# The last batch of an attention written apart, its output summed by pairs, and the next stage's table computed before the barrier

## What is computed

```python
x = layernorm(x + attention(x, Wq, bq, Wk, bk, Wv, bv, Wo))   # 16 heads of 64, block-causal mask
logits = x @ router_w.T + router_b
topv, topi = top_k(logits, 2); gates = softmax(topv)            # 2 of 8 experts for each row
y = sum over experts e of gates[e] * down_e(silu(gate_e(x)) * up_e(x))
x = layernorm(x + y)
```

## Time and profile before

| what | value |
|---|---|
| median of three runs | 1634.45 us |
| the profiled execution's own time | 1633.04 us |
| its span, first to last instruction | 1631.2 us |
| mean granted TensorE clock | 0.942 of full |
| TensorE / VectorE / ScalarE / GpSimd busy | 85% / 66% / 55% / 40% |
| first attention | to about 668 us |
| first routed experts, from the barrier | 675.6 to 894 us |

### The profile page before, as it was taken

The page is one execution under the profiler, slowest core; times in us unless marked ns, Lnnn a source line. Parts: engine busy times, 40 slices in busy tenths (PEclk is TensorE's granted clock), DMA queues, the critical chain, the costliest instruction groups (busy, mean ns, idle before and its releaser), DMA issues. The chain is left out here.

```text
span 1631.2 us, 35670 instructions
## 1 busy us (share of the span) xinstructions
PE 1392.3 (85%) x10839; PEld 1132.1 (69%) x10840; DVE 1077.9 (66%) x3450; ACT 895.7 (55%) x2391; POOL 647.9 (40%) x978
## 2 busy tenths in 40 slices
PE   5999999999999998299998269999999998988840
PEld 4777777777777777188887157777777776778740
DVE  4777777777777776266665358888888874833326
ACT  3656666666666665055554136777666766832213
POOL 1344444444444444133333232344445333325542
PEclk9999999999999999599999559999999999999975
DMA  6112020202020200011111621022214000023214
GB/s 219 52 36 72 20 73 19 73 19 73 19 73 19 74 22 13 21 42 47 48 46 38 215 67 53 30 73 73 74 47 150 7 15 15 14 67 83 79 59 126
DMA packets 59992, 96.36 MB, mean 59 GB/s; under 512 B 11140, under 2 KB 49412, under 8 KB 57432
## 3 DMA queue, kind: packets, MB, share of 16 engines
q1 hardware_dynamic: 50632, 76.47, 15.3%
q0 software_dynamic: 8864, 18.43, 3.3%
q10 hardware_dynamic: 432, 0.66, 0.1%
HBM read 75.01 MB, written 61.60 MB: 84 GB/s over the span
## 5 line engine op out<-in xcount | busy, mean ns | idle before, releaser
L362 POOL TENSOR_TENSOR a_prob<-a_prob,a_rl 128x128 f32<-128x128 f32 (+1 forms) x258 | 125.5, 508 | 256.1 <-DVE a_rl L447 255.8
L250 ACT ACTIVATE a_prob<-psum,a_nmx 128x128 f32<-128x128 f32 (+1 forms) x516 | 212.3, 423 | 11.9 <-DVE a_nmx L442 11.9
L1989 DVE TENSOR_REDUCE a_mx<-psum 128x2 f32<-128x512 f32 x256 | 170.8, 689 | 41.8 <-PE psum L1320 38.1
L276 ACT ACTIVATE a_probt<-psum 128x768 f32<-128x768 f32 x128 | 103.9, 811 | 118.9 <-PE psum L639 118.9
L1680 ACT ACTIVATE a_prob<-psum 128x1024 f32<-128x1024 f32 x128 | 129.2, 1025 | 13.8 <-PE psum L1352 13.2
L441 DVE TENSOR_REDUCE a_nmx<-psum 128x2 f32<-128x256 f32 x130 | 55.2, 425 | 118.1 <-PE psum L592 118.1
L771 POOL DMA_INDIRECT yt<-m_yrow,m_dest x71 | 67.9, 956 | 158.6 <-DVE m_yrow L922 157.5
L639 PE MATMUL psum<-ident,a_prob 128*128 128x128 f32 x768 | 106.3, 275 | 14.0 <-DVE a_prob L451 14.0
L1320 PE MATMUL psum<-a_k_stk,q_stk 128*128 128x256 f32 x512 | 109.5, 312 | 3.1 <-DVE a_mx L1989 2.1
L288 ACT ACTIVATE a_ot<-psum,a_bias 128x256 f32<-128x256 f32 x128 | 61.4, 480 | 88.1 <-PE psum L665 84.2
L250 ACT ACTIVATION_READ_ACCUMULATOR a_prob<-psum,a_nmx 128x1 f32 x516 | 108.5, 210 | 0.0
(11 more groups left out here) (346 smaller groups left out, 4245.4 us busy)
## 6 DMA issues: line engine op xcount, KB each, us to landing
xs<-in_fill SPq DMA_DIRECT2D x144, 264.0 KB
a_stage<-in_w SPq DMA_DIRECT2D x16, 384.0 KB, 4.3
m_xrow<-xs SPq DMA_DIRECT2D x39, 132.0 KB
m_xrow<-xs SPq DMA_DIRECT2D x71, 66.0 KB, 1.8
a_yin<-yt SPq DMA_DIRECT2D x16, 256.0 KB, 2.8
f_yin<-yt SPq DMA_DIRECT2D x8, 512.0 KB, 4.1
yt<-m_yrow,m_dest POOLq DMA_INDIRECT x149, 2.2
a_xin<-in_x SPq DMA_DIRECT2D x17, 128.0 KB, 2.1
```

The source lines that it names most:

```text
L250: last = nc.scalar.activation(prob[:, slot, h, at], S[:, 2 * slot + h, at], ACT.Exp, bias=nmx[:, slot, q, h:h + 1], accum_out=lsum[:, slot ...
L276: nc.scalar.activation(probt[:, hp % 2], PT[:, :, 0:SW], ACT.Copy).then_inc(pt_done, 1)
L362: last = nc.gpsimd.tensor_tensor(prob[:, slot, 0, at], prob[:, slot, 0, at], rl[:, slot, 0, q:q + 1].to_broadcast(prob[:, slot, 0, at].sha ...
L1989: nc.vector.reduce_max(mx[:, :, h:h + 1], bank.rearrange("p (q k) -> p q k", q=QB), AX.X).then_inc(mx_done, 1)
```

## The change

The last batch is written apart from the loop on each engine, with `final` set (on GpSimd both batches of the last loop turn stand apart). There the transposes, copies, projections, scores, maxima and exps for a batch that doesn't exist are left out. The output of the last batch is no longer computed by one run of 16 matmuls behind all pairs: a matmul with the identity puts x into the bank at pair 6, the pairs 0 to 5 are added there, pair 6 at pair 7, and pair 7 at the end. The residual addition on VectorE goes; statistics and normalisation of the last batch read the sum from PSUM. The count matmul and `tables` move from the start of `routed0` to the end of `attention0`, behind the last `slots`; their buffers are held in `program` for both stages. The waits for `table` go.

```diff
...
                                  ).then_inc(stage_in[half], 16)
+                    if last and half:
+                        continue
                     sp.wait_ge(xres_done, i + 1)
                     sp.wait_ge(xtr_ps, i + 1)
-
-                    nxt = 0 if last and half else i + 1
-                    sp.dma_start(xin[:], x_d[bass.ds(nxt, 1)].rearrange("a p q f -> p (a q) f")).then_inc(x_in, 16)
+                    sp.dma_start(xin[:], x_d[bass.ds(i + 1, 1)].rearrange("a p q f -> p (a q) f")).then_inc(x_in, 16)
 
...
-            def batch(i, first):
+            def batch(i, first, final=False):
                 for hp in range(HP):
                     s = i * HP + hp
-                    act.wait_ge(nmx_done, s + 2)
-                    exps((hp + 1) % 2, 0)
+                    more = not final or hp + 1 < HP
+                    if more:
+                        act.wait_ge(nmx_done, s + 2)
+                        exps((hp + 1) % 2, 0)
...
-                    if hp == 5:
+                    if hp == 5 and not final:
                         act.wait_ge(xtr_ps, i + 2)
                         activations()
...
-                    exps((hp + 1) % 2, 1)
+                    if more:
+                        exps((hp + 1) % 2, 1)
...
             batch(0, True)
-            with act.Fori(1, B) as i:
+            with act.Fori(1, B - 1) as i:
                 batch(i, False)
+            batch(B - 1, False, True)
             routed_columns(B)
             routed_ranks(B)
...
-                first, second = isinstance(j, int) and half == 0, isinstance(j, int) and half == 1
+                whole = isinstance(j, int)
+                first, second, last = whole and i == 0, whole and i == 1, whole and i == B - 1
                 for hp in range(HP):
                     if hp == 1 and not first:
                         power(i)
-                    scale((hp + 1) % 2, i * HP + hp + 2)
+                    if not last or hp + 1 < HP:
+                        scale((hp + 1) % 2, i * HP + hp + 2)
                     if hp == 0 and not (first or second):
                         scatter_rows(i - 1, 1)
...
             batch(0, 1)
-            with pool.Fori(1, B // 2) as j:
+            with pool.Fori(1, B // 2 - 1) as j:
                 batch(j, 0)
                 batch(j, 1)
+            batch(B // 2 - 1, 0)
+            batch(B // 2 - 1, 1)
             scatter_rows(B - 1, 1)
             power(B)
             keep_rows(B)
...
+                variances(res)
+
+            def variances(rows):
+                for q in range(QB):
+                    last = nc.vector.bn_stats(stats[:, q, :], rows[:, q, :])
...
-            def layernorm(n):
+            def layernorm(n, rows=res):
                 dve.wait_ge(rstd_done, n)
                 dve.wait_ge(kept, n)
                 for q in range(QB):
-                    last = nc.vector.tensor_scalar(nrm[:, q, 0:P], res[:, q, :], mv[:, q, 0:1], rstd[:, q:q + 1],
+                    last = nc.vector.tensor_scalar(nrm[:, q, 0:P], rows[:, q, :], mv[:, q, 0:1], rstd[:, q:q + 1],
                                                    ALU.subtract, ALU.mult)
...
+            def tables():
+                t = g.t0
+
+                wide = lambda a: a.unsqueeze(1).to_broadcast([P, TAB, E0])
+                dve.wait_ge(count_ps, 1)
+                chain.done(nc.vector.tensor_tensor(t.count[:], VO[:, 0:E0], rc("eoff"), ALU.subtract))
...
+                chain.done(nc.vector.tensor_scalar(t.in_at[:], t.row[:], float(XROWS - P), None, ALU.min))
...
-            def batch(i, first):
+            def batch(i, first, final=False):
                 for hp in range(HP):
                     s = i * HP + hp
-                    normalise((hp + 1) % 2, 0, s * 2 + 3)
-                    maxima(hp % 2, s + 3)
+                    more = not final or hp + 1 < HP
+                    if more:
+                        normalise((hp + 1) % 2, 0, s * 2 + 3)
+                    if not final or hp + 2 < HP:
+                        maxima(hp % 2, s + 3)
...
-                    if hp == 5:
+                    if hp == 5 and not final:
                         activations(i * 2 + 4)
                     if hp == 7 and not first:
                         slots(i)
-                    normalise((hp + 1) % 2, 1, s * 2 + 4)
+                    if more:
+                        normalise((hp + 1) % 2, 1, s * 2 + 4)
                     if hp == 0 and not first:
                         residual(i)
                     if hp == 1 and not first:
                         layernorm(i)
-                    evac_qk(hp + 3, s + 4)
-                    evac_v(hp + 3, s + 4)
+                    if not final or hp + 3 < HP:
+                        evac_qk(hp + 3, s + 4)
+                        evac_v(hp + 3, s + 4)
 
...
-            with dve.Fori(1, B) as i:
+            with dve.Fori(1, B - 1) as i:
                 chain.loop(i, LOOPED, 1)
                 batch(i, False)
-            chain.end(B)
-            residual(B)
-            layernorm(B)
+            chain.end(B - 1)
+            batch(B - 1, False, True)
+            sums = QK[:, 0:QB * P].rearrange("p (q n) -> p q n", q=QB)
+            dve.wait_ge(y_ps, B)
+            variances(sums)
+            layernorm(B, sums)
             routed_columns(B)
             logits(B)
             top_two()
             choices(B)
             slots(B)
+            tables()
...
+            def output_pairs(first, last):
+                for hp in range(first, last):
+                    for q in range(QB):
+                        end = nc.tensor.matmul(QK[:, q * P:(q + 1) * P], ot[:, hp, q * P:(q + 1) * P], wo[:, hp, :],
+                                               start=False, stop=hp == HP - 1 and q == QB - 1)
+                return end
+
...
-                    pe.wait_ge(qk_done, s + 3)
-                    scores(hp % 2, hp + 2)
+                    if not final or hp + 2 < HP:
+                        pe.wait_ge(qk_done, s + 3)
+                        scores(hp % 2, hp + 2)
...
-                    pe.wait_ge(v_done, s + 3)
+                    if not final or hp + 2 < HP:
+                        pe.wait_ge(v_done, s + 3)
+                    else:
+                        pe.wait_ge(ot_done, s + 1)
...
+                    if final and hp == 6:
+                        pe.wait_ge(xres_done, B)
+                        pe.wait_ge(ot_done, s + 1)
+                        nc.tensor.matmul(QK[:, 0:QB * P], g.ident[:], xres[:].rearrange("p q n -> p (q n)"), start=True, stop=False)
+                        output_pairs(0, 6)
+                    if final and hp == 7:
+                        output_pairs(6, 7)
+                    if final and hp + 3 >= HP:
+                        continue
...
                 batch(i, False)
-            pe.wait_ge(qk_done, B * HP + 3)
-            output(B * HP + 1, y_ps)
+            batch(B - 1, False, True)
+            pe.wait_ge(ot_done, B * HP + 1)
+            output_pairs(HP - 1, HP).then_inc(y_ps, 1)
             pe.wait_ge(nrm_done, B)
             rows_to_columns(nrm, ntr_ps)
             pe.wait_ge(nt_done, B)
             router(B)
             pe.wait_ge(lg_done, B)
             ranks(B)
+            nc.tensor.matmul(VO[:, 0:E0], g.ones[:], g.cum[:, QB * 2, :], start=True, stop=True).then_inc(count_ps, 1)
 
 
 def routed0(nc, ctx, g, d):
 
...
-            sp.wait_ge(table, 1)
...
-            nc.tensor.matmul(Y[:, 0:E0], g.ones[:], g.cum[:, QB * 2, :], start=True, stop=True).then_inc(count_ps, 1)
-            pe.wait_ge(table, 1)
...
-                dve.sem_inc(table, 1)
...
-            tables()
...
```

More of the change, by code:

```diff
@@ L182, in attention0 @@
     stage_free = sem("stage_free")
-    lg_ps, lg_done, oh_done, cum_done, rank_ps, rk_done, idx_done = (sem(n) for n in (
-        "lg_ps", "lg_done", "oh_done", "cum_done", "rank_ps", "rk_done", "idx_done"))
+    lg_ps, lg_done, oh_done, cum_done, rank_ps, rk_done, idx_done, count_ps = (sem(n) for n in (
+        "lg_ps", "lg_done", "oh_done", "cum_done", "rank_ps", "rk_done", "idx_done", "count_ps"))
     zeroed, scattered, kept, pool_cum = sem("zeroed"), sem("scattered"), sem("kept"), sem("pool_cum")
@@ L507, in slots @@
                 nc.vector.tensor_copy(idx[:], slot[:]).then_inc(idx_done, 1)
+            def tables():
[3 more added lines that the diff above has]
+                chain.done(nc.vector.tensor_tensor(t.count[:], VO[:, 0:E0], rc("eoff"), ALU.subtract))
+                chain.done(nc.vector.tensor_tensor(t.more[:], t.count[:].unsqueeze(2).to_broadcast([P, E0, NT // P]),
+                                                   rc("thr").unsqueeze(1).to_broadcast([P, E0, NT // P]), ALU.is_gt))
+                chain.done(nc.vector.reduce_sum(t.blocks[:], t.more[:], AX.X))
+                chain.done(nc.vector.tensor_tensor(t.below[:], t.blocks[:].unsqueeze(1).to_broadcast([P, E0, E0]),
```

(42 more changed lines are left out.)

26 lines of the change are left out of this document (removed).

## The result

| | before | after |
|---|---|---|
| median of six runs | 1635.55 us (1631.11 to 1642.68) | 1621.52 us (1619.74 to 1625.49) |
| profiled execution, its own time | 1633.04 us | 1621.79 us |
| its span | 1631.2 us | 1620.0 us |
| mean granted TensorE clock | 0.942 | 0.945 |

The time is 0.9921 of before, 95% interval 0.9902 to 0.9941: 12.9 us less, 9.6 to 16.0. 1623.3 was predicted against a median of 1634.45, 11.1 less. From profile to profile the span fell by 11.2.

A forecast was written before the change was run, and what follows sets the result against it. One serial chain from the first attention's last batch to the routed experts was taken to bound the handover, no engine being full. 4.0 + 7.4 - 0.3 = 11.1 us off 1634.45 gave 1623.3 us, range 1620.5 to 1629.0.

The forecast's parts named there:

- Part 1: Last batch of the first attention: dropping work for a missing batch and summing output by pairs gains 4.0 us, bounds 3.0-4.6.
- `rstd` waits for the scatters: Last batch: rstd still waits for the previous batch's four scatters, at about 649.1, the output sum ready 0.45 us earlier.
- Reading PSUM: Last batch's statistics and normalisation read PSUM instead of SBUF; the normalisation behind rstd loses 0.1 us, bounds 0 and 0.2.
- The x matmul: Last batch: the added identity matmul that puts x in the bank takes 0.3 us, bounds 0.24 and 0.65.
- Part 2: End of the first attention: the table beside the last scatters gains 7.4 us, bounds 5.9-7.8, less 0.3 for slower scatters.
- rival 3: Last four scatters: each waits out two table operations on the shared port, 3.2 us in all; 1626.2 us, chance 0.10.
- The cover: Behind the last scatter: GpSimd's idle time before the next block hides the table with 6.8 us to spare.
- Rival 1: Last batch: something else holds the slots, so they come no earlier and only the table is gained; 1627.3 us, chance 0.08.
- rival 2: Behind the barrier: the table's 7.8 us hid the next block's code arriving, so moving it gains nothing; 1630.6 us, chance 0.08.
- Rival 4: Last batch and behind the barrier: written-out code stalls at up to 2.4 us a stop, eight giving 1642.5 us; chance 0.04.
- The sum: Whole kernel: 4.0 for the last batch plus 7.4 for the table less 0.3 for scatters gives 11.1 us gained.
- What follows is unchanged: Everything behind the handover starts earlier but is unchanged, TensorE at its lower clock at the first routed block either way.

The follow-up runs named there:

- e2: The changed kernel with the table put back at the start of the routed experts (last batch's change alone): 0.9963 of the kernel before, handover 43.76 us.
- e9: The changed kernel run once more, unchanged: 0.9933 of the kernel before, handover 36.96 us.
- e5: The changed kernel with the table held until GpSimd's program has passed its last scatter: 0.9945 of the kernel before, handover 36.57 us.
- e6: The changed kernel with the same table computed three times in a row: 0.9972 of the kernel before, handover 44.34 us.
- e11: The changed kernel without the sum by pairs: 16 output matmuls behind all pairs, residual and statistics from SBUF: 0.9946 of the kernel before, handover 41.03 us.
- e10: The changed kernel with output matmuls spread over three idle gaps, slots at pair 6, table held behind GpSimd's last scatter: 0.9900 of the kernel before, handover 35.17 us.
- e1: The kernel before with only the count matmul and table moved to the end of the first attention: 0.9928 of the kernel before, handover 41.46 us.
- e8: The changed kernel with x and output matmuls spread over three idle gaps, ranks in another bank, slots at pair 6: 0.9920 of the kernel before, handover 35.88 us.
- e4: The changed kernel with x and ten output matmuls at pair 5, two at pair 6, ranks in another bank: 0.9926 of the kernel before, handover 38.26 us.
- e7: The changed kernel with 16 unread filler transposes on TensorE and the last batch's slot operations at pair 6: 0.9953 of the kernel before, handover 35.89 us.

## Why the prediction held

- **Part 1, 4.0 predicted.** e2 gives 4.67, of which 4.53 stand at `rstd`. The indices come 4.52 earlier where I took 4.1. Pair 6's transposes start 2.60 behind the mask matmul, as taken (2.62); from there to the indices' end are 3.89 (634.44 to 638.33), and I had taken 4.25 (637.6 to 641.85). That term was mis-sized; the mechanism was right.
- **`rstd` waits for the scatters.** Right in e9, e2 and six others. In e9, e2, e5 and e6 the variance ends 0.31 to 0.33 before it; where the variance releases, `rstd` starts 0.08 behind it in the profile after, so it had 0.24 to spare, against the predicted 0.45. One term of this was mis-sized: from the sum's end to `rstd` I kept 1.35, and the profile after has 1.10 (13.88 to 14.98). The 1.91 from which I took it ended with a wait for the scatters. In the profile after it failed: the output sum ended at 645.72 by the clock there, which is 13.88 behind the mask matmul; the predicted 647.3 was 12.32 behind its own (634.98), and e9 has 12.41. What failed in that execution is an unstated premise, that TensorE keeps full clock through the last batch. It cost 1.2 at `rstd`.
- **Reading PSUM, 0.1 taken.** From `rstd` to the transposes of the normalised rows are 1.54 in e9, 1.42 in e11 and 1.41 before, which read SBUF: 0.12 to 0.13.
- **The x matmul, 0.3 taken.** Two records over 0.70 at full clock, 0.5 between its start and the first output matmul's (632.88 and 633.41 in e10), 1.0 at the lower level. Too small, but beside the scatters' wait it cost nothing.
- **Part 2, 7.4 predicted, less 0.3.** e1 gives 6.97 against 7.1. From the last scatter's start to the first load are 9.43 to 9.64; the terms of the prediction give 9.2 (8.79 to the next block and 0.4), its two times 9.4. The scatters' starts spread over 3.98 or 4.58 instead of 3.91, so the added cost is 0.07 with 0.2 more behind a last scatter of 1.15, or 0.67: around the 0.3, and far from **rival 3**'s 3.2. The table ended 1.21 (after) to 1.87 (e9) behind the last scatter's start, under the predicted 2.5.
- **The cover, 6.8 predicted, is 5.85 to 6.30** (e6, e9, after), since the barrier and SP need 1.92 behind VectorE's end, and the prediction let the table run up to the barrier.
- **Rival 1** falls with e2, **rival 2** with e1: no code had hidden behind the table, the load came at once. (Its time took 3.9 off where part 1 has 4.0.) **Rival 4** too: the written-out batch has no stop for code on the chain, and its pairs keep the predicted pace or better it (2.60 and 3.89 for 2.62 and 4.25). The Trainium skill ("Runtime: NRT & Kernel Launch", section on instruction fetch mechanics) has straight code fetched ahead, and the traces agree.
- **The sum, 11.1.** e9 shows 11.47 in the handover, the profile after 9.91; 11.1 lies between them: part 1 was 0.67 too small, and the 1.56 that the clock and the long scatter took in the profile after weren't in it but for the 0.3. The measured 12.9 (9.6 to 16.0) contains both; what it has above them I can't assign, for the start of the kernel and its rest move by more than this between executions.
- **"What follows is unchanged"** wasn't exact: from the first load to the end are 947.79 before, 949.64 after, 948.40 in e1 and 948.38 in e2, and 945.39 to 952.74 in the others outside e9's chip. This is no part of the change that I could find.

Not tried: a second buffer of normalised rows, so that `rstd` of the last batch need not wait for scatters at all. After e8 this wait is worth at most 0.9 (12.29 less the variance's end at 11.32 and the 0.08 behind it).

## What to carry to other kernels

At a handover that is one serial chain, the gain of a change can be read off the links, if each is measured from an instruction ahead of it that the change hardly reaches; spans alone mixed in 3 us from the kernel's start. Work of the next stage that needs only early results belongs beside the slow end of this one, and how much fits is measured by repeating it. Moving work into an engine's idle time pays only if nothing that leads to the releasing wait is queued behind it: here ten matmuls in one gap made H 1.3 longer, and four in each of three places delayed nothing.

## What the runs showed of the hardware

The first 36 us differ between executions, whatever the kernel. The stretch from 24 to 36 us, in the kernel before, in e1 (whose code up to there is that of before), and after:

```profile
24.00:36.00 12.00, 9.52 (x62) 6.53 (x60) 5.93 (x19) 5.77 (x22) 2.86 (x6) 0.72 0.38 130
```

```profile
24.00:36.00 12.00, 9.55 (x71) 7.18 (x72) 7.41 (x23) 7.21 (x27) 3.49 (x7) 0.86 0.39 135
```

```profile
24.00:36.00 12.00, 9.52 (x85) 7.11 (x84) 8.18 (x25) 8.10 (x30) 3.99 (x9) 1.00 0.48 154
```

The granted clock was 0.72 in before, e2, e4 and e7, with pair 5's mask matmul at 634.98 to 635.75; 0.86 in e1 and e6 (632.84, 632.12); 1.00 in the other seven profiles (631.33 to 632.48). The difference arises at the start: the first scatter of all comes at 104.05 before and at 100.61 after, 3.44 apart. In the rows themselves, five of the six projection matmuls (L96 to L98) around 22 us take 0.39 to 0.42 before and 0.28 after, though the clock column shows 1.00 there in both, so the column doesn't show all of it. The mask matmul behind them starts 0.74 later before than after (24.56 and 23.82), the next one 2.13 later (30.35 and 28.22). An execution that starts on a slow TensorE is some 3 us longer for it, more than most steps weighed here. The Trainium skill ("TensorE: Matmul & The Clock Gate", Part 1) puts such a warm-up below 1% of a usual kernel's span; 3.1 of 1631 is 0.2%, and the trace agrees.

A reader who compares two profiles of one execution each must take this out first: here it would have added about 3.1 to a handover gain of 9.91.
